# Windows in pairs over one base, and the first layer's selections kept for the second layer

## The reference

```python
# layer 0; layer 1 is the same with other weights and constants
xj0, xj1 = split(node_features[dst])            # 64 scalars, 32 x 3 vectors, per edge
m0 = (xj0 * dist) @ w000 + <xj1, r_vec> @ w110  # scaled; + xj0 @ lm0
m1 = outer(xj0 @ w011, r_vec) + (xj1 @ w101) * dist   # + xj1 @ lm1
agg = segment_sum(concat(m0, m1), src)          # by node
x = layernorm(x + x + tensor_product(x, agg) + linear(x))
```

## Time and profile before

| | us |
|---|---|
| median of 3 runs | 8,750.87 |
| lowest and highest run | 8,738.81, 8,771.03 |
| the profiled execution | 8,732.45 |
| its span, first to last instruction | 8,730.6 |
| VectorE busy | 7,042.0 (81%) |
| TensorE busy | 6,827.3 (78%) |
| GpSimd busy | 4,432.0 (51%) |
| ScalarE busy | 2,872.1 (33%) |
| last message product of stage A starts at | 2,736.5 |
| last message product of stage B starts at | 6,138.4 |

### The profile page before, as it was taken

How to read it: one execution, slowest core, us unless ns; L and a number is a source line. 1 busy time by engine, 2 the same in 40 slices (tenths; PEclk the granted TensorE clock), 3 DMA queues, 4 the chain that set the end, 5 groups by cost and what they waited for, 6 DMA issues and landing times.

```text
span 8730.6 us, 145242 instructions
## 1 busy us (share of the span) xinstructions
PE 6827.3 (78%) x38863; PEld 5107.1 (58%) x38863; DVE 7042.0 (81%) x9196; ACT 2872.1 (33%) x9562; POOL 4432.0 (51%) x3371
## 2 busy tenths in 40 slices
PE   2666666666665988989898899888688888888888
PEld 1554445544444666666666676666465665656655
DVE  2656556556566989999999999987699999999999
ACT  1222222222221233333333333333344444444443
POOL 0666666666665467667676767666322222222222
PEclk5777777777777999999999999999899989999998
DMA  5556556555552455555555555554212112112111
GB/s 137 167 164 168 168 164 168 165 164 168 164 164 89 137 168 171 168 169 174 171 172 167 171 169 172 169 165 130 84 64 70 69 63 70 69 63 70 68 65 49
DMA packets 987616, 1162.81 MB, mean 133 GB/s; under 512 B 78738, under 2 KB 881553, under 8 KB 961933
## 3 DMA queue, kind: packets, MB, share of 16 engines
q10 hardware_dynamic: 460746, 590.81, 22.2%
q0 software_dynamic: 154640, 281.49, 11.4%
q1 hardware_dynamic: 372147, 289.51, 11.0%
HBM read 480.47 MB, written 681.01 MB: 133 GB/s over the span
## 4 chain that ended last, share of the span: by engine, by line
SPq 26%; PE 22%; DVE 20%; issue 15%; DMA 12%; ACT 3%; ACTq 2%; DVEq 1%; POOL 0%; POOLq 0%
SPq L423 11%; DMA table<-tab 10%; SPq L419 7%; PE prods_ps L1094 4%; PE turn_ps L1118 4%; DVE work L887 4%; PE node_ps L1127 4%; PE m_ps L1031 3%; DVE upd L893 2%; DVE work L871 2%; PE node_ps L1031 2%; DVE pick L746 2%; DVE pick L744 2%; DVE rank L747 2%; PE s_ps L1014 2%
## 5 line engine op out<-in xcount | busy, mean ns | idle before, releaser
L534 POOL DMA_INDIRECT slots<-pay,slot x3136 | 3307.9, 1055 | 1598.8 <-issue 818.6
L591 POOL TENSOR_TENSOR q<-xt,yv 125x3072 f32<-125x3072 f32 x200 | 1097.7, 5489 | 2591.3 <-PE turn_ps L1118 2562.6
L1031 PE MATMUL m_ps<-win,pick_n 125*128 125x160 f32 x4704 | 1073.0, 357 | 807.6 <-ACT pay L1284 737.0
L1095 PE MATMUL prods_ps<-w_bil,ys_t 64*125 64x512 f32 x2400 | 1472.7, 712 | 0.0
L1031 PEld LDWEIGHTS m_ps<-win,pick_n 125*128 125x128 f32 x4704 | 772.6, 214 | 1143.2 <-ACT pay L1284 867.9
L887 DVE TENSOR_TENSOR work<-prods_ps,yv 125x1024 f32<-125x1024 f32 x1200 | 1392.8, 1216 | 11.2
L893 DVE TENSOR_REDUCE upd<-work 125x48 f32<-125x3072 f32 x400 | 1341.3, 3353 | 13.6
L871 DVE TENSOR_TENSOR work<-prods_ps,xt 125x1024 f32<-125x1024 f32 x800 | 970.7, 1220 | 305.0 <-PE prods_ps L1095 291.7
L1118 PEld LDWEIGHTS turn_ps<-ident,q 125*128 125x128 f32 x9600 | 1111.3, 192 | 177.4 <-issue 152.2
L1127 PEld LDWEIGHTS node_ps<-msgs,onehot 128*125 128x125 f32 x6800 | 1009.5, 201 | 338.8 <-DMA spill_in<-spill_sums 231.4
L1127 PE MATMUL node_ps<-msgs,onehot 128*125 128x160 f32 x6800 | 1058.2, 318 | 181.9 <-DMA spill_in<-spill_sums 170.8
(11 more groups left out here) (216 smaller groups left out, 8515.7 us busy)
## 6 DMA issues: line engine op xcount, KB each, us to landing
msgs<-slots ACTq DMA_DIRECT2D x200, 1428.0 KB, 6.2
slots<-zero ACTq DMA_DIRECT2D x183, 1443.8 KB
win<-table SPq DMA_DIRECT2D x1568, 78.1 KB
table<-tab SPq DMA_DIRECT2D x200, 390.6 KB
slots<-pay,slot POOLq DMA_INDIRECT x3136
spill_sums<-zero_rows ACTq DMA_DIRECT2D x88, 180.0 KB
spill_in<-spill_sums SPq DMA_DIRECT2D x200, 78.1 KB
rec<-edge_recs SPq DMA_DIRECT2D x196, 64.0 KB, 8.0
```

Of the source, the lines that this page charges most:

```text
L534: g.indirect_dma_start(out=slots[layer][:, :], out_offset=bass.IndirectOffsetOnAxis(ap=slot[q][:, j:j + 1], axis=0), in_=pay[q][:, j, :], ...
L591: g.tensor_tensor(q3[0:HM, :].rearrange("p (i u v) -> p i u v", i=3, u=V), xt[nb][0:HM, S:D].rearrange("p (u i) -> p i u", i=3).unsqueeze( ...
L1031: mm = te.matmul(to[:, D * j:D * j + D], pick_n[hh][0:WROWS, P * (2 * p + j):P * (2 * p + j) + P], win[q][0:WROWS, p, :], start=True, stop ...
L1095: te.matmul(prods_ps[r % 2][0:HM, 512:1024], ys_t[S:P, :], w.bil[S:P, 512 * r:512 * r + 512], start=True, stop=True).then_inc(s["prods"], 1)
```

## The change

1. Four blocks share one base, the first `dst` of the third block. Blocks 3 and 4 use the window of 25 nodes from the base on, blocks 1 and 2 the one that ends at the base (24 nodes lower). One DMA of 2 x 125 rows loads both. The table gets 24 zeroed rows at each end, which SyncE stores before the first window load.
2. The selection is laid out as (node, channel) instead of (channel, node).
3. In stage A SyncE stores each half's turned selection `pick_n` to memory (`picks`, 125 rows of 4,096 bytes); ScalarE waits for the store of the chunk before (`picks_kept`) before it overwrites `pick_n`. In stage B VectorE's `select`, TensorE's `turn_pick` and ScalarE's `pick_out` are gone; `load_windows` of layer 1 also loads the stored selection into one of four buffers `pick_b`.
4. In stage B messages use two banks, `m_ps` and `s_ps`.
5. In stage B the table store goes to the end of SyncE's step, for tile t-2.

```diff
-    table = [nc.dram_tensor(f"table{layer}", [N, CHANNELS * D], F32).ap() for layer in range(2)]
+    table = [nc.dram_tensor(f"table{layer}", [EDGE + N + EDGE, CHANNELS * D], F32).ap() for layer in range(2)]
+    picks_d = nc.dram_tensor("picks", [UNITS, WROWS, UB * P], F32).ap()
-        pick_e = [sb(f"pick_e{h}", [P, UB, CHANNELS, WIN]) for h in range(2)]
-        pick_n = [sb(f"pick_n{h}", [P, UB * P]) for h in range(2)]
+        pick_b = [sb(f"pick_b{q}", [P, UB * P]) for q in range(4)]
+        pick_n = pick_b[0:2]
+        pick_e = [z[:, 0:UB * WROWS].rearrange("p (j n c) -> p j n c", j=UB, c=CHANNELS) for z in pick_b[2:4]]
...
                 for hh in range(2):
                     q = 2 * cb + hh
-                    at = [sp.value_load(base_i[0:1, bass.ds(8 * c + 4 * hh + p, 1)], min_val=0, max_val=N - WIN) for p in range(PAIRS)]
+                    at = [sp.value_load(base_i[0:1, bass.ds(4 * c + 2 * hh + p, 1)], min_val=0, max_val=N - 1) for p in range(QUADS)]
                     if within(c, 2, NCH):
                         sp.wait_ge(s["msg"], 8 * c + 4 * hh - 12)
-                    for p in range(PAIRS):
-                        sp.dma_start(win[q][0:WROWS, p, :], table[layer][bass.ds(at[p], WIN), :].rearrange("n (c f) -> c n f", c=CHANNELS)
-                                     ).then_inc(s["win_in"][q], 16)
+                    for p in range(QUADS):
+                        rows = table[layer][bass.ds(at[p], EDGE + WIN), :]
+                        both = bass.AP(rows.tensor, rows.offset, [[D, WROWS], [EDGE * CHANNELS * D, 2], [1, D]], runtime_checks=rows.runtime_checks)
+                        sp.dma_start(win[q][0:WROWS, 2 * p:2 * p + 2, :], both).then_inc(s["win_in"][q], 16)
+                    if layer == 1:
+                        sp.dma_start(pick_b[q][0:WROWS, :], picks_d[bass.ds(2 * c + hh, 1)].rearrange("u r e -> (u r) e")).then_inc(s["win_in"][q], 16)
...
             def chunk(k):
                 ...
                     load_windows(0, later(k))
+                for hh in range(2):
+                    sp.wait_ge(LS[0]["pick_out"], 4 * c + 2 * hh + 2)
+                    carry()
+                    sp.dma_start(picks_d[bass.ds(2 * c + hh, 1)].rearrange("u r e -> (u r) e"), pick_n[hh][0:WROWS, :]).then_inc(picks_kept[hh], 16)
                 if within(c, 0, NCH - 2):
                     load_recs(0, later(later(k)))
...
                 if layer == 0:
-                    if within(t, 3, NT + 3):
-                        store_table(1, (t - 3, half - 1 if b == 1 else half - 2, 1 - b))
                     if within(c, -1, NCH - 1):
                         load_windows(1, later(chunk))
...
                 if layer == 0 and within(c, -2, NCH - 2):
                     load_recs(1, later(later(chunk)))
+                if layer == 0 and within(t, 2, NT + 2):
+                    store_table(1, (t - 2, half - 1, b))
...
-                chain(ve.tensor_tensor(base, dv.rearrange("p (k a) -> p k a", a=2)[0:1, :, 0], so.bound[0:1, c0 // 2:(c0 + cols) // 2], ALU.min))
+                chain(ve.tensor_tensor(base, dv.rearrange("p (k a) -> p k a", a=4)[0:1, :, 2], so.bound[0:1, c0 // 4:(c0 + cols) // 4], ALU.min))
...
+                chain(ve.tensor_scalar(quads[:, :, 0:2], quads[:, :, 0:2], float(EDGE), None, ALU.add))
...
-                        messages(1, chunk, hh, p, (m_ps,))
+                        messages(1, chunk, hh, p, (m_ps, s_ps))
...
                 if part == 0 and within(c, 1, NCH):
                     ac.wait_ge(s["msg"], 8 * c + 4 * hh - 4)
+                    ac.wait_ge(picks_kept[hh], 16 * c)
```

More of the change, by code:

```diff
@@ L246, in build @@
         tx_in = [sem(f"tx_in{b}") for b in range(2)]
-        dma_go, sp_go = sem("dma_go"), sem("sp_go")
+        dma_go, sp_go, edges_clear = sem("dma_go"), sem("sp_go"), sem("edges_clear")
+        picks_kept = [sem(f"picks_kept{h}") for h in range(2)]
         flag_ready, spills_turned, squared = sem("flag_ready"), sem("spills_turned"), sem("squared")
@@ L429, in store_table @@
                 sp.wait_ge(s["t_out"], m + 1)
-                sp.dma_start(table[layer][bass.ds(m * HM, HM), :], tab[b][0:HM, :]).then_inc(s["t_stored"][b], 16)
+                sp.dma_start(table[layer][bass.ds(m * HM + EDGE, HM), :], tab[b][0:HM, :]).then_inc(s["t_stored"][b], 16)
+            sp.wait_ge(zero_made, 2)
+            for layer in range(2):
+                for n in (0, EDGE + N):
+                    sp.dma_start(table[layer][n:n + EDGE, :].rearrange("n (c f) -> (n c) f", c=CHANNELS), zero[0:EDGE * CHANNELS, 0:D]
+                                 ).then_inc(edges_clear, 16)
             for m in range(LEAD - 1):
@@ L450, in _ @@
             chunk_sweep(sp, chunk)
+            for hh in range(2):
+                sp.wait_ge(picks_kept[hh], 16 * NCH)
+            sp.wait_ge(LS[0]["pick_turned"], 4 * NCH)
+            sp.wait_ge(LS[0]["msg"], 8 * NCH)
             for q in range(4):
@@ L852, in node_step @@
                 s = LS[layer]
-                nodes, following = within(t, 1, NT + 1), layer == 0 and within(c, -1, NCH - 1)
+                nodes = within(t, 1, NT + 1)
                 n, nb, nh = t - 1, 1 - b, half if b == 1 else half - 1
@@ L956, in spread_base @@
                     te.wait_ge(edge_made, pc)
-                te.matmul(s_ps[:, 0:cols // 2], ones_f[0:1, :], so.base[0:1, 0:cols // 2], start=True, stop=True).then_inc(spread, 1)
+                te.matmul(s_ps[:, 0:cols // 4], ones_f[0:1, :], so.base[0:1, 0:cols // 4], start=True, stop=True).then_inc(spread, 1)
             te.wait_ge(iotas, 11)
@@ L1021, in messages @@
                 s, q = LS[layer], 2 * cb + hh
-                if p % 2 == 0:
+                loads = QUADS + layer
+                if p % 2 == 0 and layer == 0:
                     te.wait_ge(s["pick_out"], 4 * c + 2 * hh + p // 2 + 1)
                 if p == 0:
-                    te.wait_ge(s["win_in"][q], 16 * PAIRS * ck + 16 * PAIRS)
+                    te.wait_ge(s["win_in"][q], 16 * loads * ck + 16 * loads)
                 before = 8 * c + 4 * hh + p + 1 - len(banks)
@@ L1329, in node_step @@
                 units = layer == 0 and within(c, 0, NCH)
-                def out(hh, part):
-                    if units:
-                        pick_out(1, chunk, hh, part)
                 def paid(hh, p):
                     if units:
-                        pay_out(1, chunk, hh, p, (m_ps,))
+                        pay_out(1, chunk, hh, p, (m_ps, s_ps))
                 def where(hh):
@@ L1409, in node_step @@
                 turned_q(1)
-                out(1, 0)
                 linear_out()
@@ L1414, in node_step @@
                     table_turned(1, m)
-                out(1, 1)
                 paid(1, 1)
```

53 lines of the change are left out of this document (22 added, 31 removed).

## The result

The changed kernel took 9,851.65 us in the median of 4 runs (9,810.75 to 9,858.02), beside 8,748.44 us for the kernel before on the same chip: a ratio of 1.1247, 95% interval 1.1210 to 1.1284. The profiled execution's span is 9,850.9 us, 1,120 us longer than before. The forecast was 10,010 us, its range 8,900 to 10,700.

The account below looks back on a forecast made before the run. The prediction took five DMA engines, full in stage A and nearly full in stage B, as the bound. 8,732 + 833 (A) + 428 (B) = 9,993, given as 10,010 us; range 8,900 to 10,700.

Parts of the forecast that it names:

- A: Stage A, first layer's chunks alone: pick stores lengthen 26.0 us per chunk to 34.5, +8.5, +833 us in all.
- the five: The five DMA engines that 125-row transfers use; claimed full in A before the change, their packet load summing to 1.05.
- rival 2: Pick blocks run on all 16 engines: A +2.7 us per chunk, B -0.5 per step, 8,965 us; chance 0.08.
- the step named as the likeliest to fail: In A, reading the 1.05 packet sum as full engines, though packets of different queues might overlap more.
- B: Stage B, first layer's nodes beside second layer's chunks: pick loads lengthen 33.3 us per step to 37.7, +4.4, +428 us.
- the division by A's 1.048: In B, 39.5 us of packets per step, with A's overlap of 1.048, become 37.7 us.
- what the change saves in SyncE's loop: SyncE's four fewer issues and value loads, 5.6 us per period: SyncE stops being critical, and the five stand behind it.
- Rival 1: SyncE is the bound and the five only look full; A and B get shorter, about 8,190 us; chance 0.13.
- 9.0 us of SyncE's wait per step go: In B, moving the table store to the step's end removes SyncE's wait for just-stored table rows, 9.0 us per step.
- The DMA share of A rises: Test in A: the DMA share rises though GB/s per engine doesn't; no size given.
- rival 4: Record loads land behind pick stores, windows and picks behind the table store: +4.4 us per period, 10,870 us; chance 0.06.
- Windows in pairs, and selections and turns in B, worth 0: Paired window loads: 0 on the five. VectorE's 2.7 and TensorE's 2.5 us per step in B: 0 under DMA.

Follow-up runs that it names:

- e1b: Changed kernel with pick blocks of 128 rows instead of 125, in store and load; 1.0078 of the kernel before, first kind of chip.
- e7: Kernel before with only stage B's table store for tile t-2 moved to the end of SyncE's step; 8,603.59 us, 0.9867 of the kernel before.
- e2: Changed kernel with `pick_n` turning over four buffers instead of two; 1.0212 of the kernel before, second kind of chip.
- e9: Changed kernel with each zero fill of 100 rows cut into 96 and 4 rows; 1.1217 of the kernel before, first kind of chip.
- e5: Changed kernel without pick blocks and second message bank, the second layer selecting and turning again; 0.9882 of the kernel before, second kind of chip.
- e10: Changed kernel with pick blocks of 128 rows and fills cut into 96 and 4 rows; 1.0866 of the kernel before, first kind of chip.

## Why the prediction was right, and where it wasn't

- **Direction, mechanism, A: right.** 34.5 us forecast, 35.3 measured. That the five are full in the changed kernel's A is shown by two independent edits: pick blocks moved off (6.2 us; the prediction's own difference between its forecast and rival 2 is 5.8) and fills moved off (2.7 us; 2.9 expected). That they were full before, the step named as the likeliest to fail, rests on the same sum (1.05, beside 1.04 to 1.06 in three kernels of other periods); no edit took load off the five of the kernel before.
- **The total is closer than its parts.** A came 104 us dearer than forecast (937 against 833), B some 245 us cheaper (183 against 428). That these errors partly cancel is luck.
- **Rival 2's price was right in A**, for the kernel that it describes: e1b has A at 29.0 (28.7 was worked out). In all it takes 8,801 us where 8,965 was worked out, since its B is 30.7 and not 32.8. For 125 rows the rival was wrong, by the 31.8%.
- **B: the term was mis-sized**, +4.4 us per step against 2.1 measured. Against e1b the loads' own share was right (4.9 worked out between forecast and rival 2, 4.8 measured): both levels lie some 2 us too high. The step that made them so is the division by A's 1.048, taken as B's limit too: B runs at 1.09 in the changed kernel and at 1.19 in e1b, so 1.048 is no limit there. With it the prediction put what the change saves in SyncE's loop at 0, as covered by full engines. In e7 1.4 us came from the loop's order at unchanged bytes; the rest, some 0.8, wasn't isolated. The best reading is that B isn't held by the five alone but by SyncE's serial loop, whose landings and issues stretch with the load on the five; the chain fits it (44.2% table landing), and no experiment shows it apart. Rival 1 had the right engine for B, and the wrong sign for the time.
- **"9.0 us of SyncE's wait per step go": wrong.** It grew to 11.4, and e7 shows the same 11.4 from the move of the store alone. The step was read as a list with an end, not as a loop.
- **"The DMA share of A rises": wrong**, 0.59 fell to 0.53. Five engines stay full while the period grows, so the other eleven idle more. That follows from the prediction's own mechanism: (0.59 x 26.0 + 8.9 x 5/16) / 34.5 is 0.53. The sign of the test was not worked out.
- **Latency (rival 4)**: present, since e2 gets 1.9 us per chunk back, but most of it is the same shortage seen from a wait: records take 19.8 us to land in the changed kernel and 5.6 in e9, where only the fills moved.
- **Windows in pairs, and selections and turns in B, worth 0**: neither was tried alone on the first kind. On the second, the windows with the new layout go with 1.3 us per chunk less (e5), and on top of e5 picks of 128 rows with the second bank take 1.5 us per step off B.

## What to carry to other kernels

Count engine time per DMA engine, not per queue: where the busiest subset is full while the mean share is 0.59, a new transfer costs its bytes over that subset (that is A here; B followed no such sum), and padding it to a row count that spreads (125 to 128 here) can pay: 2.4% more bytes in these blocks took 10.7% off the changed kernel's time (9,852 to 8,801 us). Read an instruction queue in a loop as a ring: moving a step to the end moves it past only what lies between the old and the new place around the ring. And price an extra DMA issue by what stands behind the issuing engine, not by its median.

## What was not expected of the hardware

- A chip of the second kind takes 1.12 times as long for the kernel before (9,753 beside 8,744 us), nearly all of it in A and B: stage C has 25.2 us per step on both. TensorE's stalls there are 1.5 us in the mean, 2.9 at most. The change is 12.5% slower on one kind and 4.3% on the other; padded picks are 0.8% slower on one and 1.7% faster on the other.
- The second of two fills in a row, 57.8 KB, holds ScalarE's issue up to 10.2 us in e10's B, where a fill alone issues in 0.33 us.
- SyncE's window issues stretch in the same way where the five are full: four took 21.75 us in the changed kernel, from 1,982 us on. In A they have 2.56 us in the median there, half as many issues as before with twice the rows, beside 0.85 us before.

```profile
1982.26 21.75 SPq L432 DMA_DIRECT2D win<-table  x4
```
